# Three graph attention layers on one core: loops written out, another order of work in the last layer, input fetched in parts

## What is computed

```python
h = (x @ W.T).reshape(n, H, D)
h_src, h_dst = h[src], h[dst]
enc = relu(edge_attr @ edge_W.T + edge_b).reshape(-1, H, D)
alpha = einsum('ehd,hd->eh', h_src, a_src) + einsum('ehd,hd->eh', h_dst, a_dst)
alpha = alpha + sum(enc * h_dst, axis=-1)
alpha = where(alpha >= 0, alpha, 0.2 * alpha)
ex = exp(alpha - segment_max(alpha, dst)[dst])
out = segment_sum(h_src * (ex / segment_sum(ex, dst)[dst]), dst) + bias
```

## Time and profile before

| | us |
|---|---|
| median of 3 runs | 2442.32 |
| fastest and slowest of them | 2439.75, 2443.36 |
| the profiled execution's own time | 2431.28 |
| its span, first to last instruction | 2429.4 |

### The profile page before, as it was taken

How to read it: one execution, slowest core, us unless ns; L and a number is a source line. 1 busy time by engine, 2 the same in 40 slices (tenths; PEclk the granted TensorE clock), 3 DMA queues, 4 the chain that set the end, 5 groups by cost and what they waited for, 6 DMA issues and landing times.

```text
span 2429.4 us, 49749 instructions
## 1 busy us (share of the span) xinstructions
PE 1753.2 (72%) x8878; PEld 1055.8 (43%) x8879; DVE 1844.4 (76%) x5643; ACT 1018.6 (42%) x3430; POOL 1535.4 (63%) x1675
## 2 busy tenths in 40 slices
PE   4368777778765677777787667778777777787783
PEld 3245444444433354444454433444444444444441
DVE  5478888888896566666666766888888888888888
ACT  2233444344424354454454443444444444444444
POOL 2567777777745777777777474565555555655553
PEclk9578888888868788888887776788787787888876
DMA  5644444444612444544446122333333333333321
GB/s 153 150 129 133 139 139 143 137 136 138 192 35 72 131 131 131 137 131 132 136 131 175 57 71 79 86 107 92 91 103 86 104 89 94 107 88 97 102 69 54
DMA packets 145430, 273.39 MB, mean 113 GB/s; under 512 B 55607, under 2 KB 80306, under 8 KB 145289
## 3 DMA queue, kind: packets, MB, share of 16 engines
q0 software_dynamic: 64704, 182.91, 27.6%
q1 hardware_dynamic: 77452, 86.16, 11.8%
q10 hardware_dynamic: 3158, 3.20, 0.4%
HBM read 255.35 MB, written 17.20 MB: 112 GB/s over the span
## 4 chain that ended last, share of the span: by engine, by line
PE 30%; DVE 27%; issue 19%; POOL 9%; DVEq 6%; ACT 4%; DMA 4%; SPq 2%; POOLq 0%; ACTq 0%
PE bank L1485 15%; POOL rows L1128 7%; DVE sums L766 5%; PE bank L1499 5%; PE bank L1419 3%; DVE prod L772 3%; DVE dots L778 3%; DVE rows L755 3%; DVEq L787 3%; PE bank L1496 2%; DMA rows<-table,index 2%; DVEq L766 1%; ACT rows L1273 1%; DVE adsum L639 1%; DVE onehotT L629 1%
## 5 line engine op out<-in xcount | busy, mean ns | idle before, releaser
L1128 POOL DMA_INDIRECT rows<-table,index x1221 | 1190.4, 975 | 636.6 <-PE bank L1485 321.6
L1485 PE MATMUL bank<-rows,onehot 128*128 128x264 f32 (+1 forms) x2640 | 1015.6, 492 | 198.2 <-DVE sums L766 143.6
L766 DVE TENSOR_TENSOR sums<-sums,bank 128x264 f32 (+1 forms) x1320 | 552.6, 419 | 190.8 <-PE bank L1485 139.2
L1485 PEld LDWEIGHTS bank<-rows,onehot 128*128 128x128 f32 x2640 | 510.1, 230 | 380.3 <-DVE sums L766 207.2
L1273 ACT ACTIVATE rows<-rows,wgt 128x33 f32<-128x33 f32 (+2 forms) x1520 | 443.9, 369 | 0.2
L1280 ACT ACTIVATE prod<-bank 128x256 f32<-128x256 f32 x440 | 168.3, 383 | 408.3 <-PE bank L1499 406.9
L1228 ACT CAST onehot<-bank 128x768 f32<-128x768 bf16 x240 | 178.0, 743 | 331.5 <-PE bank L1419 328.6
L1499 PE MATMUL bank<-late,onehotT 128*128 x1320 | 259.8, 314 | 0.0
L755 DVE TENSOR_TENSOR rows<-rows,wgt 128x260 f32<-128x260 f32 (+2 forms) x560 | 240.1, 429 | 3.6 <-ACT wgt L1266 3.6
L772 DVE TENSOR_TENSOR prod<-prod,bank 128x256 f32<-128x256 f32 x440 | 182.5, 415 | 46.6 <-ACT prod L1280 43.7
L1419 PE MATMUL bank<-identb,onehotT 128*128 128x128 bf16 x1320 | 160.0, 278 | 37.3 <-DVE onehotT L629 30.5
(11 more groups left out here) (196 smaller groups left out, 1937.7 us busy)
## 6 DMA issues: line engine op xcount, KB each, us to landing
locb<-loc_d SPq DMA_DIRECT2D x120, 352.0 KB
rows<-table,index POOLq DMA_INDIRECT x1221
flags<-flags_d SPq DMA_DIRECT2D x520, 27.5 KB
table<-rows SPq DMA_DIRECT2D x25, 136.0 KB, 1.7
table<-rows SPq DMA_DIRECT2D x25, 134.0 KB, 2.4
late<-table SPq DMA_DIRECT2D x1, 3300.0 KB, 18.0
table<-rows SPq DMA_DIRECT2D x25, 129.5 KB, 2.0
late<-table SPq DMA_DIRECT2D x1, 3212.5 KB, 18.3
```

What stands on the lines that cost most here:

```text
L766: done(v.tensor_tensor(a, a, ps_sum[l][s % len(ps_sum[l])][:, 0:VV], ALU.add), "add")
L1128: g.indirect_dma_start(out=rows[:, t.u, s, 0:ROW[l]], out_offset=None, in_=table[l], in_offset=bass.IndirectOffsetOnAxis(ap=index[:, t.u, ...
L1485: done(m.matmul(ps_sum[l][s % nb][:, 0:VV], onehot[:, t.u, s, :], rows[:, t.u, s, 0:VV], start=True, stop=True), "agg")
```

## The change

It has these parts.
- Loops: `batches` and SP's `meta` are written out for all 40 batches of each layer; batch numbers are constants, and the `index` ring with its DMA is gone.
- Layer 2, two tiles for each feature instruction: `FACES` makes six groups of a batch's 11 tiles (five of two, one of one). TensorE writes the encoded features of a group to one bank (`ps_enc`) and the destinations' features to one of two others (`ps_hdst`); relu, multiply and head sum take 128 x 512. `faces(k)` says at which tile each group stands, and `dot` stands one tile behind `encode`.
- Layer 2, positions and owners: `AT[2]` puts links at 2, finish at 5, exp at 6, weightsT at 7, weights at 8; `hot` works for t+4; `hotT` and `hotP` have a position for each half. `OWNER[2]` gives VectorE three tiles instead of five, ScalarE three instead of two, GpSimd five instead of four. On TensorE the chain's steps stand ahead of the tile's sum; on VectorE ahead of the weighting.
- Sum banks rotate over all tiles instead of beginning anew in each batch.
- Opening of layer 2: batch 0 is encoded, then batch 1 in groups between the steps of batch 0's chain, and batch 2's groups inside the body of batch 0.
- Opening of layer 0: `edge_parts` stands before `scores_out`, the clearing of `sums` behind the first `hot`, the split of the edge weights behind the chain of batch 0.
- Input: x comes in six parts of four blocks; parts 0 and 1 are issued at the start, each other one as a block is stored. Edge weights and biases move from SP's queue to ScalarE's, behind its stores; the padding of the destinations is a memset; the padded edge features come later on SP's queue.
- `meta` is split: `early` fetches `locb` and `attrT` under a wait of its own.

The core of the diff:

```diff
+FACES = ((0, 2), (2, 4), (4, 6), (6, 8), (8, 10), (10, B))
+G = len(FACES)
-OWNER = ("VAVVAVAVVVV", "VAAAAAAAAAA", "AVPVVPAVPVP")
+OWNER = ("VAVVAVAVVVV", "VAAAAAAAAAA", "AVAPVPPVPPA")
-XFIRST = 6
+XPART = 4
-    dict(tops2=0, links=1, finish=4, mask=10, scores=8, tops=10, hot=0, load=7, encV=1,
-         link=3, exp=5, weights=7, hotT=1, copy=9, encA=1,
-         endsT=1, cols=4, weightsT=5, hotP=1, adst=1, scoresT=9, encP=1),
+    dict(tops2=0, links=2, finish=5, mask=10, scores=8, tops=10, hot=6, load=4,
+         link=3, exp=6, weights=8, hotT=(2, 5), copy=9,
+         endsT=1, cols=4, weightsT=7, hotP=(1, 4), adst=3, scoresT=9),
+def faces(k):
+    if k == 0:
+        late = ((6, 0), (7, 1), (8, 2), (9, 3), (10, 4), (10, 5))
+        return [(i, 2, i) for i in range(G)] + [(p, 3, i) for p, i in late]
+    return [(p, k + 3, i) for i, p in enumerate((0, 2, 4, 6, 8, 9))] if k + 3 < K else []
...
+        def sum_bank(l, t, s):
+            return ps_sum[l][(t.k * B + s) % len(ps_sum[l])]
         def batches(eng, body):
-            loops = (K - 3) // RING
-            with eng.Fori(0, loops) as j:
-                for u in range(RING):
-                    body(Batch(j, u), K)
-            for k in range(loops * RING, K):
+            for k in range(K):
                 body(Batch(k // RING, k % RING), K - k)
...
# VectorE
+                def dot(t, i):
+                    n = t.k * G + i
+                    lo, hi = FACES[i]
+                    w = (hi - lo) * D
+                    need(dve, "enc", n + 1)
+                    need(dve, "encp", n + 1)
+                    done(v.tensor_tensor(prod[:, i % 2, 0:w], prod[:, i % 2, 0:w], ps_hdst[i % 2][:, 0:w], ALU.mult),
                          "prod")
...
# SP
+                def early(t, l=l):
+                    if t.k >= RING:
+                        need(sp, "hot", l * K + t.k - 2)
+                        if l == 2:
+                            need(sp, "encp", (t.k - 2) * G)
...
# GpSimd
-                    if old:
-                        need_apart(pool, (s_index[l][t.u], t.j * 16))
...
# ScalarE, opening of layer 0
+            def fetch(i):
+                lo, hi = i * XPART, (i + 1) * XPART
+                nc.scalar.dma_start(nodes[:, lo:hi, :], x[lo * P:hi * P, :].rearrange("(b p) f -> p b f", p=P)
+                                    ).then_inc(s_x[i], 16)
+            fetch(0)
+            act.wait_ge(s_dst, 32)
+            act.wait_ge(s_w0, 16)
+            act.wait_ge(p_pool, 5)
+            fetch(1)
...
# TensorE
                 def sum_slot(t, s, l=l, VV=VV):
-                    need(pe, "add", (l * K + t.k) * B + (s - nb + 1 if s >= nb else 0))
+                    need(pe, "add", i + 1 - len(ps_sum[l]))
+                def encode(t, i):
+                    need(pe, "enc", n)
+                    lo, hi = FACES[i]
+                    for s in range(lo, hi):
+                        r = m.matmul(ps_enc[:, (s - lo) * D:(s - lo + 1) * D], attrT[:, t.u, s * P:(s + 1) * P],
+                                     edgew3[:, :], start=True, stop=True)
+                    done(r, "facep")
+                    need(pe, "prod", n - 1)
+                    for s in range(lo, hi):
+                        b = pe.snap(regs[t.u][s], min_val=0, max_val=BLOCKS - 1)
+                        for j in range(3):
+                            r = m.matmul(ps_hdst[i % 2][:, (s - lo) * D:(s - lo + 1) * D],
+                                         onehotT[:, t.u, s * P:(s + 1) * P],
+                                         hnode3[:, bass.ds(b, 1), j, :].rearrange("p a f -> p (a f)"),
+                                         start=(j == 0), stop=(j == 2))
+                    done(r, "encp")
```

More of the change, by code:

```diff
@@ L1530, in period @@
-                    if left > 3 and l == 2:
-                        for s in range(B - AT[l]["encP"], B):
-                            encode(n3, s)
-                need(pe, "tad", l + 1)
-                if l == 2:
+                        if l < 2:
+                            small(t, s, left)
+                            continue
+                        if t.k == 0 and s == 5:
+                            load(n3)
+                        for p, k, i in faces(t.k):
+                            if p == s:
+                                encode(Batch(k // RING, k % RING), i)
```

422 lines of the change are left out of this document (236 added, 186 removed).

## The result

The changed kernel takes 2274.74 us (median of 4 runs, 2272.87 to 2275.83) where the kernel before took 2441.03 beside it: a ratio of 0.9319, interval 0.9303 to 0.9335. The forecast was 2271; by the medians 166 us were saved of the 171 forecast.

The account below looks back on a forecast made before the run. GpSimd's gathers were taken to bound layers 0 and 1, VectorE to lead in layer 2. Savings of 10 + 20 + 1 + 22 + 117 + 1 = 171 us from the 2442 median gave 2271 us, range 2220 to 2335.

Parts of the forecast that it names:

- Loops, layer 2: Layer 2: written-out batches cost batch 36's 21.42 us instead of 23.19, saving 1.77 us a batch, 62 us.
- Loops, layers 0 and 1: Layers 0 and 1: GpSimd's gather pace stays, layer 1 gains nothing, layer 0 gains its excess waits, 17 us.
- the sharing term: Layer 2: one more GpSimd weighting slows VectorE through shared memory, 0 to 0.6 us a batch, taken as 0.2.
- Links and masks: Layer 2: new positions remove 0.56 us of L772's wait and L689's 0.24 a batch; the register load keeps its wait.
- TensorE: Layer 2: two-tile encodings delay the sums, costing 0.3 us a batch, bounds -0.3 and 1.5.
- (b): Layer 2: TensorE takes over at a clock of 0.80, 20.9 us a batch, saving 133, 2309 us; chance 0.16.
- Opening of layer 2: Start of layer 2: interleaved encoding starts batch 1 near 1498 instead of 1520.30, 22 us saved, bounds 10 and 28.
- Rival (e): Start of layer 2: the gathers hide the interleaved opening, so 12 of its 22 us go; no chance of its own.
- Opening of the kernel: Before layer 0's first gather: less input ahead of the 128 KB vector shortens VectorE's wait, 10 us saved, bounds 0 and 15.
- (a): Only the loops pay: layer 2 batch 21.4 us, saving 115, 2327 us; chance 0.14.
- (c): Layer 2: denser work raises the clock and hides the register load, 18.6 us a batch, saving 219, 2223 us; chance 0.10.
- (d): All layers: straight code isn't fetched in time and stalls the batches, slower at 2530 us; chance 0.05.

Follow-up runs that it names:

- the controls: The kernel before and the changed kernel, both unchanged, run again on one chip: 2447.2 and 2277.72 us, ratio 0.9333.
- the first pair: The two profiled executions behind the result, kernel before and changed kernel: spans of 2429.4 and 2272.3 us.
- The kernel with cut instructions: The changed kernel with each two-tile relu, multiply and head sum cut into two instructions of 256: 0.9275 of the kernel before, on the slower chip.
- the link rows late: The changed kernel with one more weighting of layer 2 on ScalarE instead of VectorE (two, four, five tiles): 2302.95 us, ratio 0.9441.
- its old-opening form: The changed kernel with layer 2 opened as before, three batches encoded ahead of batch 0's scores: 2281.84 us, ratio 0.9340.
- the last experiment: Kernel with tile 0 on VectorE (three, three, five), GpSimd's layer 2 weightings moved between gather groups of the batch before: 2238.17 us, ratio 0.9170.

## Why the prediction was right, and where its steps were off

The total (171 us) was near the 166 of the medians; by stages it was near the controls (173) and 14 too high against the first pair. That difference lies in the baseline: the profiled execution of before was a fast one, and the changed kernel's profiled execution (2274.25 us) does not lie under its median. The sum was closer than its terms: the openings and the gathers of layer 0 gave less than forecast, layer 1 gave 5 us that weren't forecast, and in layer 2 a clock that wasn't counted on made up for a price that was too low. Adding the 11 us to the forecast was right, since the changed kernel had to be set against the median.

*Loops, layer 2.* The price from one pair of numbers, 1.77 us, measured 1.37: 48 us instead of 62. Batch 36 was no cheap one, as its 21.42 us is near the 21.49 of the 31 ordinary batches with the loops written out. What one batch couldn't show is the four of 25 us, with the stretched scan and the lower clock: they make 0.40 of the mean of 21.90.

*Loops, layers 0 and 1.* Layer 1 gains nothing from them, as said, and layer 0 10 to 14 us instead of 17. The changed kernel's idle time in layer 0 fell by 14.4 us and the three slow gathers near 101.99 are gone, but the gathers behind got longer by 6.5 (16 ns each): in the changed kernel 38 of these 407 take over 1.21 us, in the kernel before one. While 25 of the 39 over 1.2 us run, VectorE builds the one-hots (L647) or takes the difference ahead of the exponential (L745), against 53 of the other 368. That is an association; the cause is open. The 4.9 us of layer 1, which were not forecast, are shorter gathers (955 against 966 ns); loops alone leave them at 966, so something else in the change brings them. The index that no longer comes from a ring is a candidate, not tried.

*Two tiles per instruction.* The new form lasts 678 ns and the next instruction starts 0.6 us after it, as estimated from the 692 of L386. VectorE's work was forecast at 17.6 us a batch and is 616.86 / 35 = 17.6. That holds for all the parts together; no run gives the time that the pairs alone are worth.

*Owners.* The sign of the sharing term, 0.2 us, was right. Against before the link steps got longer by 0.47 us a batch (573, 702 and 421 ns against 454, 454 and 320), but the scan L695 got shorter by 0.12 and the one-hots by 0.05 (618 to 573 ns), which leaves 0.3. Against a kernel in which the link steps lie clear of GpSimd they are 0.8 to 0.9 longer. The Trainium skill ("GPSIMD Engine Reference", Key points) names as contending VectorE's instructions with two inputs in SBUF or in a two-port mode; the traces agree, as the scans and weightings with two SBUF inputs got longer while the multiply, with one input in a bank, hardly did: 421 ns in the 24 cases in the kernel before that lay wholly beside a weighting, 414 in the others. The copy L710 with its one input got longer too, 153 to 573; whether it runs in a two-port mode no trace shows. Pricing "one weighting more" missed the point: what counts is whether the block of weightings lies over VectorE's steps. The kernel with cut instructions has five weightings as well and short link steps, so the fifth one alone doesn't decide it.

*Links and masks.* The prediction put L766's 1.40 us down to the register load, but its row names TensorE's bank for 40.1 of the 49.1 us; the register load shows as the 21.2 us of "issue" at L784 in the changed kernel, 0.6 a batch and not the 0.93 that the lower bound of the period was made with. L689's wait went, as said. The wait ahead of the multiply fell from 30.8 us to 18.9, 0.34 us a batch of the 0.56 counted, and it is now for TensorE's destination features. The stretch of order as a whole (pairs, owners, places) was put at 1.52 us a batch (21.42 to 19.9) and measured 2.04 (21.90 to 19.86).

*TensorE.* This is the term that was mis-sized, and here luck came in. I took its time as given, at a clock of 0.80, and charged 0.3 us for it. Its matmuls ran at 0.95 and its busy time fell by 1.9 us a batch, so it had room for the pair encodings. What the clock is worth can be read inside the changed kernel, whose batches did not all run at the same one. Two neighbours:

```profile
1579.57:1599.09 19.52, 15.28 (x100) 9.13 (x98) 17.65 (x46) 10.89 (x38) 13.44 (x17) 1.00 0.40 114
1599.09:1620.10 21.01, 17.99 (x100) 10.99 (x98) 17.76 (x46) 10.90 (x38) 13.74 (x16) 0.84 0.37 105
```

Of its 35 batches, 22 ran at 1.00 throughout and took 19.50 us on average, and nine at 0.84 to 0.86 took 20.99. Carried on to 0.80, an estimate from these two levels, a batch would take some 21.4 us, more like rival (b)'s 20.9 than the forecast's 19.9. So the sum was about 1.5 us too low for the clock that it was made at, the higher clock gave that back, and the period was right to 0.05 us for reasons that were half right. In the other orders the same step costs less: 20.49 against 19.40 us with tile 0 on VectorE, 20.38 against 19.66 with four tiles there. The clock of layer 2 went with the kernel: 0.80 before, 0.83 with the loops alone, 0.90 with the link rows late, 0.91 and 0.93 with four and three tiles on VectorE and tile 0 among them, 0.94 to 0.96 in the changed kernel, its old-opening form and the last one. Which of the parts raises it isn't separated.

*Opening of layer 2.* 22 us forecast, 14 to 15 measured. The step that failed is "some 19 us of VectorE" behind the end of the gathers: batch 0 took 27 us, and batch 1 started 27.5 us after the end of the gathers (28.5 in the control) instead of 20. The rescaling of batch 0 does start with the end of the opening gathers (1455.92 and 1454.77 in the control). Rival (e) was nearer for the interleaving taken alone: 4.6 us.

*Opening of the kernel.* 10 forecast, 4.7 and 12.7 in the pairs, 8 over all kernels. The wait for the vector fell by 5.2 us (14.95 to 9.72), not by 10.

*The rivals.* (a), only the loops pay: fell, as a batch went to 19.9 and the loops alone gave 2371 us. (b), TensorE at 20.9: fell with the clock, the condition that it named; at 0.80 it would have been the nearer one, by the estimate above. (c), 18.6 us: not in the changed kernel, but the last experiment reached 18.89; its saving adds up to 217.5 us and not 219. (d), stalls of straight code: fell; its sum took 2.1 us for 80 batches without a reason, and the 2.5 us that it states for all 120 would give 2571 us. More code was fetched, and the longest "issue" wait of VectorE in layer 2 is 1.0 us, at L784 where registers are loaded. The second instruction queue of the kernel before over 1530 to 2330 us (its first is in the earlier trace rows), then both over that stretch of the changed kernel (packets, MB, share):

```profile
q8 instruction: 2, 0.03, 0.0%
```
```profile
q8 instruction: 36, 0.59, 0.3%
q14 instruction: 50, 0.41, 0.2%
```

The Trainium skill's rule ("Runtime: NRT & Kernel Launch", Instruction fetch mechanics), straight code fetched ahead and taken branches stalling, agrees: the jump's 33.7 us at L747 went with the loops.

*The signs.* No third batch is longer, VectorE's busy time is 17.6 us and TensorE's share stays under 90%, as named. But the batches started 19.1 to 21.4 us apart, not 19.5 to 20.3, and layer 1 changed by 4.9 us, just under the 5 that were to tell against the prediction.

## What to carry to other kernels

Price each stage against what waits there: the same edit, loops written out, was worth nothing in layer 1, where GpSimd set the pace, and 1.4 us a batch in layer 2, where VectorE and a chain did; in all it was worth 72 us on one chip and 120 on another with a lower clock. When several engines share a chain, look for the steps that lie beside another engine's block and at what stands right ahead of each link; moving one block of GpSimd's work cut 25 us with no instruction less. And give TensorE's clock a term of its own: compare batches of the same kernel at either level before trusting a sum made at one.

## What was not expected of the hardware

VectorE's copy of 8 numbers took 153 ns clear of GpSimd's weightings and 573 on average in the changed kernel, where it mostly lies beside them, a scan of 96 numbers 345 and 702. A scan of 88 x 128 that takes 0.41 us lasted 3.11 beside a block of four weightings, until the block had ended. TensorE's granted clock rose from 0.80 to 0.95 of the full 2.4 GHz over 700 us when the order of its work changed and its matmuls did not. And one of the chips granted 0.70 where others granted 0.80, and the kernel before was 17% slower there; that the clock is the whole reason isn't shown.
